# A GNN and expert network on one core: in the last stage the first group's power is issued ahead of the second group's four accumulating gathers

## The reference, cut to what matters

```python
h = relu(self_term + neigh + b)            # second graph convolution
x = x + (h + xn) * 0.5                     # xn: normalized x
xf = layernorm(x)
logits = xf @ router_w
gate_vals, idx = top_k(logits, 2); gates = softmax(gate_vals)
for e in range(8):
    hid = relu(xf @ w1[e] + b1[e]) @ w2[e] + b2[e]
    y = layernorm(xf + hid, gamma[e], beta[e])
    out = out + sum(where(idx == e, gates, 0))[:, None] * y
x = x + out
```

## Time and profile before

| | |
|---|---|
| median of three runs | 2515.83 us (2512.80 to 2517.05) |
| the profiled execution: time | 2514.59 us |
| the profiled execution: span | 2512.9 us |
| busy share of the span | PE 94%, PEld 74%, DVE 70%, ACT 45%, POOL 27% |
| mean clock granted to TensorE | 0.966 of full speed |
| last stage | from about 1925 us to the end |

### The profile page before, as it was taken

How to read it: one execution, slowest core, us unless ns; L and a number is a source line. 1 busy time by engine, 2 the same in 40 slices (tenths; PEclk the granted TensorE clock), 3 DMA queues, 4 the chain that set the end, 5 groups by cost and what they waited for, 6 DMA issues and landing times. The chain is left out here.

```text
span 2512.9 us, 33394 instructions
## 1 busy us (share of the span) xinstructions
PE 2351.5 (94%) x10815; PEld 1863.4 (74%) x10818; DVE 1766.7 (70%) x4174; ACT 1133.5 (45%) x2077; POOL 685.3 (27%) x626
## 2 busy tenths in 40 slices
PE   6899895999999999999689999999996999999998
PEld 4677674777777777778567888888875677777776
DVE  7678796777787877786465765555565677777775
ACT  6564323444535454544342222222234766666652
POOL 6465013222222211210122212122233333323310
PEclk9899896999999999999899999999998999999999
DMA  5121132212121212211543343434356566666631
GB/s 168 49 61 43 42 118 97 84 51 101 55 97 57 95 68 84 82 66 51 153 138 105 130 146 125 135 132 130 129 170 194 114 154 147 152 167 146 145 100 47
DMA packets 155777, 271.89 MB, mean 108 GB/s; under 512 B 35442, under 2 KB 36082, under 8 KB 155382
## 3 DMA queue, kind: packets, MB, share of 16 engines
q1 hardware_dynamic: 122918, 203.00, 24.4%
q0 software_dynamic: 32720, 67.19, 11.4%
HBM read 185.82 MB, written 100.41 MB: 114 GB/s over the span
## 5 line engine op out<-in xcount | busy, mean ns | idle before, releaser
L2385 ACT ACTIVATE conv_h<-conv_h 128x512 f32<-128x512 f32 x79 | 50.0, 632 | 304.7 <-DVE conv_h L2314 304.7
L2845 POOL DMA_INDIRECT next_own<-message,net_slot_d x75 | 123.9, 1652 | 161.8 <-DMA next_own<-own 134.8
L2283 DVE TENSOR_TENSOR conv_yl<-conv_pty,conv_yh 128x512 fp32r<-128x512 f32 x79 | 54.6, 692 | 149.3 <-ACT conv_yh L2375 141.0
L68 PE MATMUL d_po<-shared_wq_hi,d_hh 128*128 128x512 f32 x316 | 130.8, 414 | 7.0 <-DVE d_hl L1508 3.0
L1024 POOL DMA_INDIRECT early_val<-values,net_slot_s x79 | 85.2, 1078 | 189.7 <-DVE d_x L1502 88.5
L1733 ACT ACTIVATE d_act_out<-d_pa 128x512 f32<-128x512 f32 (+1 forms) x80 | 46.1, 576 | 200.3 <-PE d_pa L70 200.3
L68 PE MATMUL conv_p<-conv_w_hi,conv_yh 128*128 128x512 f32 x316 | 132.5, 419 | 1.3 <-DVE conv_yl L2283 1.3
L68 PE MATMUL d_pa<-d_xh,xp_w_hi 128*128 128x512 f32 (+1 forms) x320 | 129.9, 406 | 0.0
L68 PE MATMUL d_pc<-d_xh,shared_wv_hi 128*128 128x512 f32 (+1 forms) x320 | 129.7, 405 | 0.0
L69 PE MATMUL d_pa<-d_xl,xp_w_hi 128*128 128x512 f32 (+1 forms) x320 | 127.0, 397 | 0.0
L70 PE MATMUL d_pa<-d_xh,xp_w_lo 128*128 128x512 f32 (+1 forms) x320 | 126.6, 396 | 0.0
(11 more groups left out here) (614 smaller groups left out, 7204.5 us busy)
## 6 DMA issues: line engine op xcount, KB each, us to landing
conv_yin<-y SPq DMA_DIRECT2D x79, 256.0 KB, 2.8
h<-conv_h SPq DMA_DIRECT2D x79, 256.0 KB, 2.0
own<-xp_own_buf SPq DMA_DIRECT2D x79, 256.0 KB, 2.0
next_own<-own SPq DMA_DIRECT2D x79, 256.0 KB, 4.6
next_x<-y SPq DMA_DIRECT2D x79, 256.0 KB, 2.9
out<-d_res SPq DMA_DIRECT2D x79, 256.0 KB, 2.6
y<-d_y SPq DMA_DIRECT2D x78, 256.0 KB, 2.0
d_x<-in_x SPq DMA_DIRECT2D x10, 1024.0 KB, 6.5
```

The lines of the kernel that those rows point to most:

```text
L68: te.matmul(out, lhs[0], rhs[0], start=first, stop=False, skip_group_check=True)
L2283: v.tensor_tensor(lo[:, t % 2, :], bank[t % 2][:], hi[:, t % 2, :].bitcast(F32), ALU.subtract)\
L2385: act_.activation(h[:, t, :], h[:, t, :], ACT.Relu).then_inc(h_made, 1)
L2845: pool.indirect_dma_start(own[n][:, t, :], None, k.message2[:, :], bass.IndirectOffsetOnAxis(ap=k.slot["d"][:, T * g + t:T * g + t + 1], a ...
```

## The change

The two calls for group 0's power and group 1's gathers change places on POOL. Nothing else in the kernel changes, and no other engine's list does.

```diff
@@ -2864,8 +2864,8 @@
                 if in_range(i, c_, 0):
                     power2(g)
 
+            power(0)
             gather(0, 1)
-            power(0)
             gather(0, 2)
             power(1)
             bodies(pool, body)
```

## The result

Over ten runs each, the changed kernel took 2522.26 us (2519.01 to 2524.41) and the kernel before 2514.32 us (2511.62 to 2517.22). The ratio is 1.003, 95% interval 1.0022 to 1.0038, that is +5.5 to +9.6 us. I had forecast +6.1 us, slower by more than 0.2% with 0.56. The changed kernel's profiled execution took 2521.32 us, its span is 2519.6 us.

The account below looks back on a forecast made before the run. PE was taken to bound the last stage's body, so only the prologue could change the time: 5.2 (landings) + 1.4 (clock) - 0.5 (early gain) = +6.1 us on the median 2515.83, giving 2521.9 us, range 2517.3 to 2525.0.

Parts of the forecast that it names:

- The power cannot start earlier by leaving the gathers behind: On POOL, group 0's power waits for DVE's variance after 2.70 us idle, so moving it ahead of the gathers saves nothing.
- The landings at the last `half` of group 2, +5.2 us: On ACT, the eighth gather lands at 1963.3, so this `half` starts 5.2 us late (bounds +1.4 and +7.8).
- The rival without a pile-up: Each gather lands 5.4 us after issue, last `half` 2.2 us late; +3.1 us in all, 2518.9 us; chance 22%.
- Group 1's own delay: On ACT, group 1's last gather lands 1.6 us late; about 1.0 us reaches the squares and group 1's power.
- The clock, +1.4 us: PE's pause before group 1's transposes grows to 7.0 us; half clock for 3.0 to 5.9 us behind it costs 1.4 us.
- The early gain, -0.5 us: Early prologue: group 0's message rows no longer meet group 1's gathers; DVE's 1.76 us wait shrinks, saving 0.5 us.
- The body carries the shift: In the last stage's body PE is busy 480.00 of 480.00 us, so a shifted beginning arrives at the end undiminished.

Follow-up runs that it names:

- busy_pe: The changed kernel plus 28 matmuls, output never read, in PE's pause before group 1's first transpose; +5.9 us against the kernel before (1.0014 to 1.0039).
- no_group1: The changed kernel with group 1's four gathers left out, so group 1 gets no messages; -0.8 us against the kernel before (0.9984 to 1.0002).
- two_ahead: The changed kernel with two of group 1's gathers ahead of group 0's power, two behind; +1.2 us against the kernel before (0.9999 to 1.0017).
- hold_loads: The changed kernel with SP's loads of group 3's `own` held until the eighth gather landed; +4.1 us against the kernel before (1.0003 to 1.0023).
- the second profile: The changed kernel run and profiled once more, unaltered; +8.1 us against the kernel before (1.0014 to 1.0037).
- late_y_power: The changed kernel with SP's y loads for group 3 issued behind group 2's `own` loads; +3.8 us against the kernel before (1.0004 to 1.0026).
- combined: late_y_two with y loads behind group 3's `own` loads and 8 extra matmuls in PE's pause; -2.3 us against the kernel before (0.9980 to 0.9998).
- late_y_two: late_y with two of group 1's gathers ahead of group 0's power, two behind; -3.4 us against the kernel before, ratio 0.9987 (0.9975 to 0.9998).
- late_y: The kernel before with SP's y loads for group 3 issued behind group 2's `own` loads; -2.0 us against the kernel before (0.9979 to 1.0002).

## Why the prediction was right

*The power cannot start earlier by leaving the gathers behind.* Right. It waits 10.27 us for the variance, and POOL was free in both orders.

*The landings at the last `half` of group 2, +5.2 us.* Right in mechanism and size: +5.0 and +5.6 us behind the power in the two profiles, +5.2 in busy_pe. The step is shown by taking the gathers away (no_group1: gone), by moving fewer of them (two_ahead: gone), and by sparing them the loads (hold_loads: halved). The count of the DMA engines' work came to 8.4 us for the eighth gather (1963.3 - 1954.9); it took 8.1 and 8.7. I had given the engines 19.3 us at a share of 0.93; from 1945.20, 2.1 us behind the first issue, to the landing at 1964.30 it is 19.1 us at 0.91:

```profile
1945.20:1964.30 19.10, 11.09 (x41) 8.13 (x39) 6.55 (x17) 12.93 (x31) 13.35 (x9) 0.68 0.91 164
```

The rival without a pile-up had +2.2 us at this step.

*Group 1's own delay.* The last `half` of group 1 was to be 1.6 us late and was 2.2, since its gather took 5.9 us to land and not 5.4. Group 1's power was 1.6 us late behind group 0's where I had 1.0. Both are covered by the later wait, as the 1.76 us of idleness ahead of that power show.

*The clock, +1.4 us.* Right in kind, and the size varies: 0.6 and 1.6 us in the two profiles of the changed kernel, 0.8 to 1.7 in the others at half clock, by the same difference to 17.76. The way of reckoning it held: 45% of the time that PE works at half clock, less what waits for DVE and ACT cover. What varies is that time. The granted clock fell in the middle of the pause, so part of the half clock passed while PE was idle. 2.7 us of it fell on PE's work in the first profile, and at least 4.7 in the second:

```profile
1973.76:1978.50 4.74, 4.74 (x13) 3.88 (x14) 3.50 (x11) 4.36 (x8) 3.30 (x3) 0.50 0.92 132
```

45% of 2.7, 4.8 and 5.1 us (hold_loads) less 0.6 us gives 0.6, 1.6 and 1.7, which is what the three lost; the 0.6 is fitted to them. I had 3.0 to 5.9 us at half clock and 0.4 to 0.9 covered. Of the pauses, my rows had one of at least 2.00 us that was not followed by half clock at once and one of at least 3.25 that was; here half clock followed 2.63, 2.89 and 2.91 us, and did not follow 1.78 and 1.80.

*The early gain, -0.5 us.* This term did not hold. It was 0.34 us in the first profile, but across six profiles with the y loads in place and none or one of group 1's gathers ahead, the power starts anywhere from 15.02 to 16.25 us, and with two or four ahead at 15.14 and 15.59. What holds the message rows are the y loads, which I had named as staying. Without it the sum for the stage is +6.6 and not +6.1; the mean of the two profiles is +6.8 (5.1 and 8.4).

*The body carries the shift.* Right: from L3299 of `body` 0 to the end it is 536.4 us before (587.9 - 51.4) and 536.3 in the changed kernel; the second profile has 1.0 us more, and two_ahead, hold_loads, late_y_power and combined 0.6 to 0.8 more. I have no cause for this part.

That the forecast of 2521.9 us lies 0.4 us from the measured 2522.26 is in part luck. It was added to 2515.83, the median of three runs; over ten the kernel before took 2514.32, and the difference is 7.9 us where I had 6.1. In the first profile the clock term was 0.8 us too large, in the second it was nearly right, and 1.0 us of the second's loss, behind `body` 0, was in no term.

The medians give +7.9 and +8.1 us, a little over what the traces hold. Between single profiles the stage of one kernel differs by 3.3 us, so two of them can't settle the last microsecond.

## What to carry to other kernels

An instruction that waits long is a bad neighbour to put ahead of DMA issues that wait for nothing: the engine's idle time ahead of it was being used. Before moving a DMA issue back, find the instruction that consumes the transfer, take the slack between landing and use, and count the DMA engines' work in the stretch into which the transfer is moved. Here two gathers fitted into the slack, three and four did not, and half of the loss came from loads of another queue that fell onto them.

## What the runs showed of the hardware that I had not expected

- An accumulating gather of 256 KB keeps the DMA engines occupied for about 1.8 us of full share (0.82 over 8.90 us for four), and eight in a row are hardly slower each than four: the eighth takes 5.8 us to land when no loads are beside it (hold_loads), against 5.4 us for the fourth of four before. With four plain loads of 256 KB beside it it takes 8.1 to 8.7 us. The Trainium skill, "DMA: Bandwidth & Descriptors", section "Queues, rings and completion order", has the engines take turns between queues; the runs agree, since loads that SP issued from 1956.3 on, behind the gathers of 1954.34 and 1956.18, delayed these: 7.3 and 8.1 us to land, 5.6 and 5.8 in hold_loads.
- Four plain loads issued 0.4 us apart beside four row gathers set the start of the whole stage's chain: with these loads issued later, the third row gather landed in 4.0 us (late_y_power) in place of 6.5 (the changed kernel, with the same order on POOL), and in late_y the power was done 2.1 us earlier.
- The granted clock was 0.50 behind a pause of PE of 2.63 us in two_ahead, 2.89 us in no_group1 and 2.91 us in late_y_two, and stayed at 1.00 over 1.78 us (before) and 1.80 us (late_y).
